# Group 0 of a DLRM tower kernel: row selection in two halves, layer 0 for the first tile alone at first

## The reference

```python
B, F, D = (512, 32, 32); LAYER_SIZE = [128, 128]
e = jnp.stack([tbl_0[ids[:, 0]], ..., tbl_31[ids[:, 31]]], axis=1)      # (B, F, D)
x0 = prev = e
for W in (filter_0, filter_1):                # (1, 32*32, 128) and (1, 32*128, 128)
    z = jnp.einsum('bhd,bmd->bhmd', x0, prev).reshape(b, h * m, d)
    prev = jax.nn.relu(jnp.einsum('bpd,pn->bnd', z, W[0]))
    outs.append(prev)
z = jnp.sum(jnp.concatenate(outs, axis=1), axis=-1)                      # (B, 256)
h = jnp.concatenate([z, dense_ctx], axis=1)
h = jnp.maximum(h @ W_top1 + b_top1, 0.0)
h = jnp.maximum(h @ W_top2 + b_top2, 0.0)
y = h @ W_top3                                                           # (B, 1)
```

## Time and profile before

| | |
|---|---|
| median of 3 runs | 855.92 us (854.44 to 856.09) |
| the profiled execution | 851.75 us |
| its span, first to last instruction | 849.9 us |
| PE, DVE, ACT, POOL busy | 831.0, 800.8, 781.9, 729.4 us |
| first matmul of layer 1 | 25.00 us into the span |
| mean granted TensorE clock | 1.000 |
| matmuls, weight loads | 3589, 3589 |

### The profile page before, as it was taken

One profiled execution on the slowest core, in us unless ns is written; L12 is line 12 of the kernel. 1 busy time (PEld: TensorE's weight loads), 2 busy tenths in 40 slices (PEclk: granted clock), 3 DMA queues, 4 the chain that ended last, 5 costly groups with the idle time before them and its releaser, 6 DMA issues.

```text
span 849.9 us, 17183 instructions
## 1 busy us (share of the span) xinstructions
PE 831.0 (98%) x3589; PEld 667.2 (79%) x3589; DVE 800.8 (94%) x863; ACT 781.9 (92%) x2770; POOL 729.4 (86%) x552
## 2 busy tenths in 40 slices
PE   4999999999999999999999999999999999999998
PEld 4677888888888888888888888888888888888875
DVE  4688999999999999999999999999999999999995
ACT  2789999999999999999999999999999999999993
POOL 6679889988888998888999888899888899988871
PEclk9999999999999999999999999999999999999999
DMA  5432323222332321233322133232122233212000
GB/s 157 127 105 85 78 83 85 83 43 50 84 78 81 84 66 37 73 78 83 82 83 49 44 84 78 82 84 77 32 68 79 80 83 84 57 37 76 1 13 1
DMA packets 62293, 60.17 MB, mean 71 GB/s; under 512 B 26395, under 2 KB 37275, under 8 KB 62270
## 3 DMA queue, kind: packets, MB, share of 16 engines
q1 hardware_dynamic: 58174, 57.80, 23.0%
q0 software_dynamic: 4096, 2.11, 3.3%
HBM read 55.51 MB, written 4.31 MB: 70 GB/s over the span
## 4 chain that ended last, share of the span: by engine, by line
PE 91%; DVE 3%; POOL 2%; issue 2%; DMA 1%; SPq 1%; ACT 0%; POOLq 0%; DVEq 0%
PE ps_y L776 26%; PE ps_y L784 26%; PE ps_y L777 25%; PE ps_c L752 3%; PE ps_c L762 3%; PE ps_c L760 2%; PE ps_c L761 2%; DVE csum L650 1%; POOL z L383 1%; PE ps_c L758 1%; DVE prod L637 1%; DMA copy_sb<-copy_of 1%; PE ps_y L803 1%; PE ps_y L796 1%; POOL z_lo L373 0%
## 5 line engine op out<-in xcount | busy, mean ns | idle before, releaser
L507 ACT ACTIVATE prod<-ps_y,es 128x128 f32<-128x128 f32 x2560 | 724.4, 510 | 32.9 <-PE ps_y L784 29.9
L650 DVE TENSOR_REDUCE csum<-prod 128x64 f32<-128x1664 f32 (+2 forms) x256 | 478.7, 1870 | 0.1
L776 PE MATMUL ps_y<-w_hi,c_both 128*128 128x512 f32 x1024 | 413.3, 404 | 1.7 <-DVE prod L637 0.8
L784 PE MATMUL ps_y<-w_hi,c_both 128*128 128x512 f32 x1024 | 399.6, 390 | 0.0
L777 PE MATMUL ps_y<-w_lo,c_both 128*128 128x512 f32 x1024 | 399.5, 390 | 0.0
L637 DVE TENSOR_TENSOR prod<-ps_y,es 128x512 f32<-128x512 f32 x384 | 256.0, 680 | 25.9 <-PE ps_y L784 23.8
L393 POOL TENSOR_TENSOR prod<-prod 128x768 f32<-128x768 f32 (+1 forms) x128 | 240.6, 1880 | 32.6 <-ACT prod L507 24.7
L776 PEld LDWEIGHTS ps_y<-w_hi,c_both 128*128 128x128 f32 x1024 | 192.4, 188 | 53.7 <-issue 7.6
L777 PEld LDWEIGHTS ps_y<-w_lo,c_both 128*128 128x128 f32 x1024 | 192.4, 188 | 47.4 <-issue 7.5
L784 PEld LDWEIGHTS ps_y<-w_hi,c_both 128*128 128x128 f32 x1024 | 192.2, 188 | 42.0
L383 POOL TENSOR_TENSOR z<-first,second 128x512 f32<-128x512 f32 x155 | 198.3, 1298 | 30.2 <-PE ps_c L758 22.2
(11 more groups left out here) (102 smaller groups left out, 273.5 us busy)
## 6 DMA issues: line engine op xcount, KB each, us to landing
second<-et_scratch SPq DMA_DIRECT2D x155, 256.0 KB, 4.1
first<-et_scratch SPq DMA_DIRECT2D x31, 256.0 KB, 3.3
et_scratch<-gat SPq DMA_DIRECT2D x62, 64.0 KB
prod<-w SPq DMA_DIRECT2D x4, 512.0 KB, 4.7
h_scratch<-h_sums SPq DMA_DIRECT2D x120, 2.0 KB
gat<-table,rows_now POOLq DMA_INDIRECT x116, 2.4
wt_sb<-wt SPq DMA_DIRECT2D x2, 512.0 KB
rows_now<-rows SPq DMA_DIRECT2D x30, 2.0 KB, 1.8
```

The costliest lines, as they stand in the source:

```text
L507: last = nc.scalar.activation(prod[:, buffer_of(g, u), h // 2, :, h % 2], ps_y[:, bank_of(g, u, k), j * N:(j + 1) * N], ACT.Copy, scale=es ...
L650: nc.vector.tensor_reduce(csum[:, g.r, maps, u], prod[:, buffer_of(g, u), fields_folded(g, u) // 2:F // 2, maps, :].rearrange("p a n t -> ...
L776: nc.tensor.matmul(out, hi, w_hi, start=True, stop=False)
L784: nc.tensor.matmul(out, lo, w_hi, start=False, stop=True).then_inc(y_ready, 1)
```

## The change

- The 128x512 selection of group 0 is cut into two halves by gathered rows: half 0 uses the rows of tiles 0 and 1 (64 of the 128 columns of `gat`), half 1 those of tiles 2 and 3. Each half has all 24 matmuls, of 64 columns each. `first` is kept in `c1_parts`. The products are made by half (`multiply_picked`).
- Layer 0 of group 0 is made for tile 0 first, in the free bank `ps_h1` (128 columns). The other three tiles (384 columns) follow: chunk 0 ahead of layer 1, the others after banks 1, 2 and 3 of tile 0.
- The warm-up is 18 matmuls on a tile of `z_lo` that DVE zeroes at the start; it waits for nothing else.
- The first DMA of `w1` goes out after `w0` and the tables. The row numbers take four steps on DVE and not five. `ones_b` comes late.
- SP stages the row numbers of group 3 ahead of the loads of groups 1 and 2, and group 1's loads of `first` and `second` no longer wait for `z_ready`.
- Group 1 is not split either (`UNSPLIT = 2`): chunks 1 to 3 of its layer 0 are one matmul in f32 each.
- ACT rounds banks 4 to 7 of `w1` after its first scaling; POOL takes the rest of banks 6 and 7. POOL issues all four gathers of group 3 in tile 2.

The pieces of the diff stand in the order SP, POOL, ACT, DVE, PE.

```diff
-WARM_UP = 10
+UNSPLIT = 2
+WARM_UP = 18
+HALF = TG // 2 * D
...
+        first_picked = c1_parts[:, :, :].rearrange("p n t -> p (n t)")
+        warm = z_lo[:, 0, :]
...
+        def half_of(x, half):
+            return x.rearrange("p (q c) -> p q c", q=BT)[:, :, half * HALF:(half + 1) * HALF]
...
-            filters(0)
             sp.dma_start(w0a_sb, w0a).then_inc(w0_in, 16)
...
-            sp.dma_start(ones_b[:, :], ones_of_b).then_inc(ones_in, 16)
-            sp.wait_ge(gathered[0], 16 * TG)
+            filters(0)
+            sp.wait_ge(gathered_first[0], 16 * TG // 2)
+            sp.wait_ge(gathered_first[1], 16 * TG // 2)
...
-                wait(sp, z_ready, g.times(KP))
-                sp.sem_inc(sp_passed, 1)
+                if not (isinstance(g.i, int) and g.times(1) == 1):
+                    sp.wait_ge(z_ready, g.times(KP))
+                    sp.sem_inc(sp_passed, 1)
...
+            sp.wait_ge(rows_step, 8)
+            sp.wait_ge(rows_past, 1)
+            stage(Group(0, SLOTS))
             for g in range(1, SLOTS):
                 pairs(Group(0, g))
-            sp.wait_ge(rows_step, 10)
-            sp.wait_ge(rows_past, 1)
-            stage(Group(0, SLOTS))
...
+            for k in (NK - 2, NK - 1):
+                pool.wait_ge(w1_hi_ready, k + 1)
+                part = slice(k * HB, (k + 1) * HB)
+                nc.gpsimd.tensor_tensor(w1_lo[:, part, :], w1_raw[:, part, :], w1_hi[:, part, :].bitcast(F32),
+                                        ALU.subtract).then_inc(w1_last_lo, 1)
...
-            Z_LO_AT_FIRST = {1: (1,), 2: (2, 3, 4)}
+            Z_LO_AT_FIRST = {2: (4,)}
...
+                gathered_at = {2: range(TG)} if number == 0 else {2: (0,), 3: (1, 2, 3)}
...
+            copy_first(0)
             round_w1((0, 1))
-            act.wait_ge(picked, 1)
-            nc.scalar.activation(first[:, :], ps_y[:, PICKS["first"], :], ACT.Copy).then_inc(first_copied, 1)
+            copy_first(1)
...
-            round_w1((2, 3, 4, 5))
-            rectify_first(slice(0, 1), first_c_hi)
-            rectify_first(slice(1, TG), c_hi_ready)
-            round_w1((6, 7))
+            act.wait_ge(l0_first, 1)
+            rectify_first(FIRST_TILE, ps_h1, first_c_hi)
+            round_w1((2, 3))
...
+                        if number == 0 and (u, k) == (0, 1):
+                            round_w1((4, 5, 6, 7))
+                        if number == 0 and (u, k) == (0, 3):
+                            act.wait_ge(l0_done, 1)
+                            rectify_first(OTHER_TILES, ps_c, c_hi_ready)
...
-            Z_HI_AT_FIRST = {(1, 1): (0, 5), (1, 2): (0, 7), (1, 3): (1, 1), (1, 4): (1, 5)}
+            Z_HI_AT_FIRST = {(1, 4): (2, 1)}
...
+            for place, k in enumerate(PICK_ORDER):
+                multiply_picked(k, place, 0)
             rest_w1(0)
             rest_w1(1)
+            for place, k in enumerate(PICK_ORDER):
+                multiply_picked(k, place, 1)
             dve.wait_ge(z_hi_ready, SPLIT)
+            rest_z(slice(0, 1), first_z_lo, 1)
             turn(Group(0, 0))
+            rest_first(FIRST_TILE, ps_h1, first_c_hi, first_c_lo)
+            rest_w1(2)
+            rest_z(slice(1, TG), z_lo_ready, SPLIT)
+            rest_w1(3)
...
+            pe.wait_ge(warm_zeroed, 1)
+            for n in range(WARM_UP):
+                nc.tensor.matmul(ps_y[:, 0, :], warm[:, 0:P], warm, start=True, stop=True)
+            pe.wait_ge(picks_in, 16 * BT)
+            for half in range(2):
+                pe.wait_ge(gathered_first[half], 16 * TG // 2)
+                for place, load in enumerate(("first",) + PICK_ORDER):
+                    if half:
+                        pe.wait_ge(*((half_z, place) if place else (first_copied, 1)))
+                    table_of, shift = {"first": (1, 0), LASTK: (1, P // 2)}.get(load) or (0, 16 * load)
+                    for q in range(BT):
+                        last = nc.tensor.matmul(half_of(ps_y[:, PICKS[load], :], half)[:, q], picks_sb[:, q, table_of, shift:shift + P],
+                                                gat[:, 0, half * HALF:(half + 1) * HALF], start=True, stop=True)
+                    last.then_inc(picked, 1)
...
             for k in range(KP):
-                layer0(Group(0, 0), k, 0)
+                last = first_layer0(k, slice(0, 1), ps_h1[:, FIRST_TILE])
+            last.then_inc(l0_first, 1)
+            first_layer0(0, slice(1, TG), ps_c[:, OTHER_TILES])
+
+            L0_REST_AT = {1: (1,), 2: (2,), 3: (3, 4)}
+            Z_USED_AT_FIRST = ((1, 3), (1, 6), (2, 2), (2, 5), (2, 7))
```

More of the change, by code:

```diff
@@ L204, in tower @@
         sp_passed = sem("sp_passed")
+        gathered_first = [sem(f"gathered_first{half}") for half in range(2)]
+        half_z = sem("half_z")
+        first_z_lo = sem("first_z_lo")
+        l0_first = sem("l0_first")
         gathered = [sem(f"gathered{s}") for s in range(SLOTS)]
@@ L248, in buffer_of, with unsplit, splits_at_once, rows_gathered @@
             return (TG * g.r + u) % BUFS
+        def unsplit(g):
+            return isinstance(g.i, int) and g.times(1) < UNSPLIT
+        def splits_at_once(g):
+            return SPLIT if unsplit(g) else 1
+        def rows_gathered(g):
+            return (g.i + (1 if g.r else 0)) * (16 * TG)
+        def half_of(x, half):
+            return x.rearrange("p (q c) -> p q c", q=BT)[:, :, half * HALF:(half + 1) * HALF]
+        def by_tile(x):
+            return x.rearrange("p (b o d) -> p o b d", b=GB, d=DT)
         def before(g, u, n=1):
@@ L798, in _ @@
-            pe.wait_ge(picks_in, 16 * BT)
-            pe.wait_ge(gathered[0], 16 * TG)
-            for load in ("first",) + PICK_ORDER:
-                table_of, shift = {"first": (1, 0), LASTK: (1, P // 2)}.get(load) or (0, 16 * load)
-                for q in range(BT):
-                    last = nc.tensor.matmul(ps_y[:, PICKS[load], q * P:(q + 1) * P], picks_sb[:, q, table_of, shift:shift + P],
-                                            gat[:, 0, :], start=True, stop=True)
-                last.then_inc(picked, 1)
@@ new lines, in first_layer0 @@
+            def first_layer0(k, tiles, out):
+                if k < LASTK:
+                    pe.wait_ge(z_ready, PICK_ORDER.index(k) + 1)
+                    return nc.tensor.matmul(out, w0_sum[:, k, :], by_tile(z[:, k, :])[:, tiles], start=(k == 0), stop=False)
+                pe.wait_ge(*((first_z_lo, 1) if tiles.start == 0 else (z_lo_ready, SPLIT)))
+                return nc.tensor.matmul(out, w0_lo[:, k, :], by_tile(z_lo[:, k, :])[:, tiles], start=False, stop=True)
+            pe.wait_ge(w_ready, 2)
@@ L829, in body @@
                             layer1(g, u, k, number)
+                        if number == 0 and u == 0:
+                            for chunk in L0_REST_AT.get(k, ()):
+                                last = first_layer0(chunk, slice(1, TG), ps_c[:, OTHER_TILES])
+                                if chunk == LASTK:
+                                    last.then_inc(l0_done, 1)
                         if more and (u, k) in z_used_at:
```

108 lines of the change are left out of this document (55 added, 53 removed).

## The result

The changed kernel takes **861.0 us** (858.84 to 862.3, six runs) beside 856.02 us for the kernel before on the same chip (six runs, 854.44 to 857.93): ratio 1.0051, interval 1.004 to 1.0063. It is slower by 5.0 us where 3.9 us less were forecast. The profiled execution took 860.73 us.

A forecast was written before the change was run, and what follows sets the result against it. PE was taken as the bound, so gains lay only ahead of layer 1 and in stalls of groups 0 and 1: 1.9 us at group 1's mark plus 2.0 behind it, 855.92 - 3.9 = 852.0 us, range 849.8 to 854.6.

The forecast's parts named there:

- the selection's term: Selection of group 0: each half's 24 matmuls take 0.2235 us each, 5.36 us a half, 10.7 us in all.
- the fast halves: Rival, selection of group 0: halves truly half as long, layer 1 from 16.3, time 848.4 us; chance 8%.
- 7.3 and 9.2: Ahead of half 0: warm-up ends at about 7.3 us if the clock rises on the way; half 0 starts at 9.2.
- The rival on the low clock: Start of half 0: clock at its low level after up to 1.9 us idle, costing 1.9 us, 853.9 us; chance 18%.
- The rival on the other side, all 48 at the low level: Selection: 64 columns or warm-up zeros do not raise the clock, +6.8 us, 862.7 us; chance 5%.
- The sum against the median: Whole kernel: 3.9 us taken off the median, which lay 4.2 us above the profiled execution: 852.0 us.
- the 3.4 us of the start: Ahead of layer 1: its first matmul starts at 21.6 us and not at 25.0, 3.4 us earlier.
- Half 0 from 9.2: Start of the selection: half 0 begins at 9.2 us, with bounds of 8.2 to 9.9.
- What comes back in, 2.1 + 0.5, mark 1 at 21.9 behind layer 1: PE: 2.1 us of layer 0 inside tile 0, 0.5 for group 1's chunks 1 to 3; group 1's mark at 43.5.
- Group 1's 2.0 us go whole: Group 1: its 2.0 us of stalls, from POOL held by late staged row numbers, vanish entirely.
- Banks 6 and 7, margin 0.3 to 0.4, costed at nothing: POOL's rests of `w1`: bank 7 ready 6.5 us after layer 1 starts, wanted at 6.9; lateness could cost up to 1 us.
- DVE and ACT as the next bound: Rival, loop: all is given back because DVE and ACT bind next, 855.9 us; chance 7%.

The follow-up runs named there:

- e13: The kernel before, word for word, run again beside other variants: ratio 1.0004 to the kernel before on the same chip.
- e14: The changed kernel with 28 warm-up matmuls in place of 18, a repeat on another chip: ratio 1.0059 to the kernel before.
- e7: The changed kernel with the staging request for group 3's row numbers back behind the loads of groups 1 and 2: ratio 1.0109 to the kernel before.
- e1: The changed kernel with its selection in one piece again, all else as changed: ratio 0.9997 to the kernel before.
- e17: The kernel before with early staging and a 28-matmul warm-up on a zeroed tile, its selection sending two signals in place of six: ratio 0.9992.
- e2: The changed kernel with the halves kept but each matmul streaming its 64 columns twice: ratio 1.0013 to the kernel before.
- e10: The kernel before with early staging and a 28-matmul warm-up on a zeroed tile, no halves: ratio 0.9973.
- e12: The changed kernel once more, word for word, on another chip: ratio 1.0058 to the kernel before.
- e16: The kernel before with early staging and a 28-matmul warm-up on a zeroed tile, a repeat on another chip: ratio 0.9966.
- e3: The changed kernel with 28 warm-up matmuls in place of 18, halves kept: ratio 1.0054 to the kernel before.
- e4: The changed kernel with its selection in one piece and 34 warm-up matmuls in place of 18: ratio 0.9992 to the kernel before.
- e9: The changed kernel with its selection in one piece and 34 warm-up matmuls, a repeat on another chip: ratio 0.999 to the kernel before.
- e5: The changed kernel with its selection in one piece, 34 warm-up matmuls and the staging request back at its old, late place: ratio 0.9969.
- e6: The kernel before with only the staging request put ahead of the loads of groups 1 and 2: ratio 0.9965.
- e18: The kernel before with the early staging alone, a repeat on another chip: ratio 0.9978.
- e8: The kernel before with only the warm-up changed, 28 matmuls on a zeroed tile from the start: ratio 0.9985.

## Why the prediction was wrong

**Where it went.** In profiles with late signals, group 2's mark is at 79.94 in the changed kernel and at 74.69 in the kernel before (e13): 5.25 us, and 5.0 lie between the medians. The start makes +5.3 of it (32.57 against 27.23), groups 0 and 1 up to the first mark +2.0 (23.0 us against 21.0), the stretch behind it -2.1 (24.36 against 26.50).

**The step that failed** is the selection's term, "each half costs 5.36 us", 10.7 us for both: it prices all 48 matmuls at TensorE's high level. At that level the price was right: a record of 64 columns took 0.115 us (e14), so a matmul 0.23, and the load of the weights bounds it, as the earlier trace rows said; the fast halves are refuted. But from 12 us on the clock was at 0.50, a record took 0.21 us, and the two halves took 18.68 us (e7; 20.4 in the changed kernel, with its stand). The forecast took the pause ahead of half 0 as harmless, although it had both numbers for it, 7.3 and 9.2. The trace has 7.5 and 9.8, and the clock fell at 11.9. It fell so in the other profiles with a pause of about that length or more too: e7 (2.25 us), e1 (3.91), e17 (1.96). After pauses of 1.41 to 1.52 us (e2, e10, e12, e16) it did not; e12 is the changed kernel itself.

The rival on the low clock (18%) named the pause but expected the low level at once and for part of half 0, at 1.9 us. In it the clock returns after 3.7 us of matmuls, as behind the warm-up of before. It did return so with 128 columns (e1, e2, e17). With 64 columns it returned before the end of the selection in none of six profiles; in e7 that was 16 us of them. The rival on the other side, all 48 at the low level (5%), gave layer 1 at 21.6 + 10.7 = 32.3, and the trace has 32.57. That it comes so near is partly luck: 20 records ran at the high level, and a start 0.6 us later, the stand of TensorE and 0.6 us more between selection and layer 1 made up for them. Its reason was half right: the zeros of the warm-up did raise the clock (1.00 from 5.07 us on), the 64 columns did not. It was not tied to the pause, and without the pause the late signals lower the clock all the same (e3, e14).

**The sum against the median.** The profiled execution of before had prompt signals and lay 4.2 us under its median; I took the difference as an offset that stays. Two things make it up. e13, late, has group 2's mark 2.24 us later than the profile of before, and its tail behind layer 1 is 2.8 us longer, since the clock does not hold there. The profile of before, with a mean clock of 1.000, was a rare one: on chip C 2 of 25 executions of that kernel had it, at 851.6 and 851.97 us. What is won ahead of 22 us is lost again where signals are late. So where signals are late, the 3.4 us of the start would not have shown even with the clock held: e4 and e9, one piece, clock held through the selection, are at 0.999.

**The other steps.** *Half 0 from 9.2:* 9.80, within its bounds. *What comes back in, 2.1 + 0.5, mark 1 at 21.9 behind layer 1:* 23.0, and 22.9 in e5, with prompt signals and the clock at 1.00, so undersized by 1.0. PE's wait of 0.3 us for `w1_lo` and the slow records right behind it are about half of that. *Group 1's 2.0 us go whole:* right in cause, and shown alone by e6, 27.05 to 24.38 us; 2.7 in place of 2.0, since the stretch between these marks is shorter than the period of 25.08 that the sum took off. *Banks 6 and 7, margin 0.3 to 0.4, costed at nothing:* PE waited 0.3 us for POOL's `w1_lo` once, so the margin was used up and a little over. *DVE and ACT as the next bound:* no sign of it; the stretch behind mark 2 is the same to 0.4 us in all profiles.

**What stays open.** What holds the signals back. They were late in the changed kernel and in e1 to e4 and e9 to e18, on four chips at least, and prompt in the profile of before and in e5 to e8, all four of which ran on one chip. The late traces hold 8,800 to 8,950 records of semaphore updates, the prompt ones 10,330 to 10,350, so fewer records and late signals go together. That could point to the path by which such events are recorded, but it is not shown. Of the 1,401 records that e13 has fewer than the profile of before, 1,184 are of DMAs that land, and they are missing all through the program, while signals are late near its start alone. And no run here shows an execution without recording. The medians go with it (before: 854.59 us on the prompt chip, 856.25 to 856.9 on the late ones), and so does e5's gain that e4 lacks. The Trainium skill, NOTIFIC — the notification-queue block, section 7.1 Overflow: three behaviours, one of which stalls the engine, says that the block's internal pipeline holds back its producers rather than lose a record inside. That would fit the waiting, though not the missing records, and no run here shows the block.

**The best version.** The kernel before with the early staging alone is at 0.9965 (e6, prompt) and 0.9978 (e18, late); with the warm-up on the zeroed tile as well 0.9973 and 0.9966 (e10, e16, both late). All four beat both kernels. Whether the warm-up adds to the staging is not shown: 0.9978, 0.9973 and 0.9966 are on three chips, and their intervals overlap. One piece, warm-up 34 and early staging where signals are prompt was never seen: from e5's mark 1 at 41.41 and 24.4 us behind it, an estimate of group 2's mark is 65.8, 6.6 us less than before.

## What to carry to other kernels

Matmuls split thinner than their weight load cost the load twice. Worse, in six profiles of six TensorE went through all that were left of them at its low level, once the clock had fallen: look at what stands right ahead of them, and let the warm-up run until the data are there. Move one queue entry before rewriting a stage: a single staging request brought 2.5 us (e6) and 1.5 us (e18), where the whole change was forecast to bring 3.9. And before a few microseconds at the start are explained by an edit, profile the kernel before on the same chip as the variants: four of them looked like proof for the early staging until they ran elsewhere.

## What the runs showed of the hardware

- The same work was seen at either level of the clock: dense 64-column matmuls in f32 went on at 1.00 for 6.4 us (e14), and at 0.50 for 15.5 us (e7). During 128-column ones it rose (e1 by 15.2, e2 by 24.9). PE and PEld show no gap in the windows of e1, e2 and e7, and next to none in that of e14.
- The pace of the 64-column records, each with its weight load, follows the clock: 0.115 us a record at the high level (e14), 0.21 at the low one (e7).
- With late signals TensorE came to stand after 51 to 56 of the 96 records of the halves, and in e18 after 44 of 48, and then went on in steps of some 0.7 or 1.4 us until about 21.8 us. In the other eight late profiles, all with the selection in one piece, its 48 records ran through. The profiles name no releaser for this stand, and its cause is open.
- Signals of TensorE that were due from 12 us on came, in fifteen of twenty profiles, as late as 22 us, and then in a burst.
